# Attention, resampling, a GRU and a coupled oscillator on one core: where VectorE splits a block of weights, and how many selection matrices it builds before q and k

## The reference, cut to what matters

```python
x = x + attention(x, cond, ...)   # 16 heads of 32: rms norm, scale and shift by cond,
                                  # qkv, rms norm of q and k, softmax, o + o @ W_out
x = x + resample(x, cond)         # every output is w0*x[i0] + w1*x[i0+1], i0 and w1 from cond
x = x + gru(cond, x, ...)         # 64 steps, one after another
x = x + oscillator(cond, cond, x, ...)  # 64 steps of RK4, one after another
```

## Time and profile before

| | |
|---|---|
| median of three runs | 1607.8 us (1606.19, 1607.80, 1607.89) |
| the profiled execution, its own time | 1608.79 us |
| its span, first to last instruction | 1606.9 us |
| mean granted TensorE clock | 0.985 of full speed |
| PE busy | 1525.0 us, 95% of the span |
| DVE busy | 1361.6 us, 85% |
| ACT busy | 942.8 us, 59% |
| POOL busy | 685.1 us, 43% |

### The profile page before, as it was taken

One profiled execution on the slowest core, in us unless ns is written; L12 is line 12 of the kernel. 1 busy time (PEld: TensorE's weight loads), 2 busy tenths in 40 slices (PEclk: granted clock), 3 DMA queues, 4 the chain that ended last, 5 costly groups with the idle time before them and its releaser, 6 DMA issues.

```text
span 1606.9 us, 95997 instructions
## 1 busy us (share of the span) xinstructions
PE 1525.0 (95%) x42395; PEld 1356.1 (84%) x42395; DVE 1361.6 (85%) x3317; ACT 942.8 (59%) x2884; POOL 685.1 (43%) x851
## 2 busy tenths in 40 slices
PE   5799999999999999699999999999999999999995
PEld 3476767777777777699999999999999999999994
DVE  6778888888888887668999898988899998989897
ACT  6567677777766765245555555555555555555553
POOL 2335555544554553533433443343443443343331
PEclk8999999999999999899999999999999999999998
DMA  6111122222222213100000000000000000000000
GB/s 220 29 55 55 56 58 55 62 62 75 71 68 68 61 36 107 34 6 14 14 15 15 15 14 13 13 15 15 15 14 13 14 14 15 14 14 14 12 15 16
DMA packets 106658, 59.88 MB, mean 37 GB/s; under 512 B 77368, under 2 KB 91872, under 8 KB 106240
## 3 DMA queue, kind: packets, MB, share of 16 engines
q1 hardware_dynamic: 106144, 53.70, 13.0%
q10 hardware_dynamic: 96, 0.02, 0.0%
HBM read 33.71 MB, written 11.60 MB: 28 GB/s over the span
## 4 chain that ended last, share of the span: by engine, by line
PE 85%; DVE 8%; issue 5%; ACT 1%; DMA 0%; POOL 0%; ACTq 0%; DVEq 0%; POOLq 0%
PE psB L1365 33%; PE psA L1394 15%; PE psQ L1083 10%; PE psA L1399 7%; PE psQ L1124 7%; PE psO L1154 5%; PE psA L1092 2%; PE psO L1142 2%; PE psB L1106 2%; DVE first L716 1%; DVE front L724 1%; DVE first L719 1%; DVE room L737 1%; PE psQ L1179 0%; DVE PT L776 0%
## 5 line engine op out<-in xcount | busy, mean ns | idle before, releaser
L1365 PE MATMUL psB<-first,Wx 128*128 128x64 f16 x9216 | 292.3, 193 | 4.7 <-issue 3.8
L1394 PE MATMUL psA<-ts,Cp 128*128 128x64 f16 x8192 | 283.7, 193 | 11.5 <-ACT ts L1433 10.9
L1365 PE MATMUL psB<-first,Whh 128*128 128x64 f16 x9072 | 286.7, 193 | 0.9
L1365 PEld LDWEIGHTS psB<-first,Wx 128*128 128x128 f16 x9216 | 279.5, 98 | 5.8 <-issue 5.5
L1365 PEld LDWEIGHTS psB<-first,Whh 128*128 128x128 f16 x9072 | 273.9, 98 | 1.8 <-issue 1.7
L1083 PE MATMUL psQ<-Wx,front 128*128 128x512 f16 x1152 | 269.7, 384 | 4.6 <-DVE front L896 3.9
L1394 PEld LDWEIGHTS psA<-ts,Cp 128*128 128x128 f16 x8192 | 258.4, 98 | 13.1 <-ACT ts L1433 11.8
L1433 ACT ACTIVATE ts<-qst 128x256 f16<-128x256 f32 x192 | 80.1, 417 | 314.3 <-DVE qst L1536 314.3
L1083 PEld LDWEIGHTS psQ<-Wx,front 128*128 128x128 f16 x1152 | 111.3, 99 | 124.2 <-issue 7.1
L1399 PE MATMUL psA<-ts,Cp 128*128 128x64 f16 x4096 | 163.2, 194 | 0.3
L1674 POOL TENSOR_TENSOR en<-rz,dn 128x256 f32<-128x256 f32 x64 | 46.7, 729 | 257.0 <-issue 256.1
(11 more groups left out here) (187 smaller groups left out, 3008.1 us busy)
## 6 DMA issues: line engine op xcount, KB each, us to landing
front<-in_x SPq DMA_DIRECT2D x32, 256.0 KB, 2.7
rows<-rows_dram SPq DMA_DIRECT2D x64, 128.0 KB, 2.9
out<-ot SPq DMA_DIRECT2D x512, 16.0 KB, 1.8
x<-x SPq DMA_DIRECT2D x31, 224.0 KB
Whh<-in_L_cond_W_qkv SPq DMA_DIRECT2D x12, 256.0 KB, 7.6
room<-in_L_cond_W_hh SPq DMA_DIRECT2D x12, 256.0 KB, 2.9
room<-in_L_cond_W_ih SPq DMA_DIRECT2D x12, 256.0 KB, 2.8
wih_dram<-front SPq DMA_DIRECT2D x12, 256.0 KB, 3.0
```

Of the source, the lines that this page charges most:

```text
L1365: last = mm(o, W_[:, i, c, g * PART:(g + 1) * PART], src[:, j, c, :], start=False, stop=False, skip_group_check=True)
L1394: mm(psF[:, s % 2, m, :], Cp[:, i, c, m * PART:(m + 1) * PART], ts_[:, 0, c, :], start=(c == 0 and m == 0 and i == 0), stop=False, skip_gr ...
```

## The change

Two edits, both in the order of DVE's list in a slot. In slots 4 to 30 one chunk of the first selection matrix, where there were two, is built before `low_qk`, and three after it; in slot 3 none before it and four after it, so that the wait for the row of indices stands behind `low_qk` too. In slots 4 to 27 `low_wr` moves from the end of the slot to between the two calls of `weigh_taps`. Nothing is removed or added, and the list of the last slot and what follows it is the same.

```diff
             if p := pair(1):
                 scale_x(p)
-            if tap:
-                build(tap, 0, (0, 1))
+            if tap and tap.n > 0:
+                build(tap, 0, (0,))
             if p := pair(-1):
                 low_qk(p, 0)
                 low_qk(p, 1)
             if tap:
-                build(tap, 0, (2, 3))
+                build(tap, 0, (1, 2, 3) if tap.n > 0 else range(KC))
             sums_qk(qk, 0)
...
             if tap:
                 weigh_taps(tap, 0)
+            if 0 <= i - WR_FROM < WR_PIECES:
+                low_wr(i - WR_FROM)
+            if tap:
                 weigh_taps(tap, 1)
             if i == 3:
                 seeds()
-            if 0 <= i - WR_FROM < WR_PIECES:
-                low_wr(i - WR_FROM)
```

## The result

| | before | after |
|---|---|---|
| median | 1607.85 us (4 runs, 1606.19 to 1608.50) | 1584.72 us (4 runs, 1584.17 to 1593.25) |
| ratio of the runs | | 0.9883, 95% interval 0.9862 to 0.9904 |
| profiled execution | 1608.79 us, span 1606.9 | 1584.21 us, span 1582.4 |
| granted clock, mean | 0.985 | 0.986 |

The change makes the kernel faster by 1.17% with an interval of 0.96 to 1.38%: 18.8 us, 15.4 to 22.2. The forecast was 18.5 us less. The two medians differ by 23.1 us, more than the interval of the ratio allows. Two later comparisons, made with the experiments, gave 0.9882 (0.9866 to 0.9898) and 0.9867 (0.9837 to 0.9897), 19 to 21 us, with medians 19.05 and 19.62 us apart.

What follows compares the result with a forecast made beforehand. PE was taken to bound the slot but for a wait at the scores, set by DVE's path; 13.0 + 0.4 + 0.96 + 4.1 = 18.5 us less gave 1589.3 us, range 1586.8 to 1595.5.

Steps and rivals of the forecast that it cites:

- The path: DVE's chain from end of sampling to scores sets the slot; PE waits 0.54 us at the scores in 24 slots.
- The move of `low_wr`: Its 0.60 us falls into DVE's 0.99 us wait for the second sampling; alone worth 0.34 a slot, 8.2 us.
- Rival A: First chunk meets POOL's L415 or ACT's high halves are late; only `low_wr` pays: 12.7 us, 1595.1, chance 0.10.
- One chunk ahead: Moving the dear second chunk behind `low_qk` frees about 1.06 us; with both edits the whole wait goes, 13.0 us.
- PE's floor: The slot without PE's wait at the scores was taken as about 18.68 us.
- slot 4: Behind `seeds()`, PE's whole wait of 0.96 us goes, bounds 0.8 and 0.96.
- Slot 3: Wait for the row of indices hidden behind PE's work: 3.4 us, up to 4.8 if the clock stays up; middle 4.1.
- The chunks behind `low_qk`: Three chunks go at the ends of POOL's instructions; `low_p` and `mix` not delayed; costed at nothing.
- Rival C: Chunks behind `low_qk` shut out until POOL's row ends: 3.9 us a slot, 1713; chance 0.03 with anything else slower.
- Rivals B and D: B: another engine partly late, 1594 to 1595, chance 0.10; D: floor not 18.68, slot 3 alone gains, 1604, chance 0.03.
- The sum: 13.0 + 0.4 + 0.96 + 4.1 = 18.5 us less over the whole kernel, 1589.3 us.

Runs made afterwards that it cites:

- experiment 1: Only `low_wr` moved between the weighings, chunks as before, against the kernel before: 1598.57 us, ratio 0.9959.
- experiment 2: Only the chunks reordered, from slot 4 on, slot 3 and `low_wr` as before, against the kernel before: 1589.65 us, ratio 0.9901.
- experiment 9: Changed kernel with `low_wr` back at the end of the slot: 1585.96 us, ratio 0.9881 to the kernel before.
- experiment 8: Changed kernel with two chunks ahead of `scale_x` and two behind `low_qk`: 1586.66 us, one run.
- experiment 7: Changed kernel with the tap indices worked out before the sums of the probabilities in slot 2: 1582.66 us, again 1584.07; ratios 0.9849 and 0.9863 to the kernel before.
- experiment 3: Only slot 3's four chunks put behind `low_qk`, all else as in the kernel before: 1602.17 us, ratio 0.9981.
- experiment 4: The changed kernel run again, nothing altered, against the kernel before: 1585.79 us, ratio 0.9882.
- experiment 5: Changed kernel with no chunk ahead of `low_qk` in any slot, all four behind: 1587.42 us, ratio 0.9871 to the kernel before.
- experiment 10: Changed kernel with each block's split (`low_wr`) done twice between the weighings: 1589.57 us, one run, beside one of before at 1609.57.

## Why the prediction held, point by point

**The path.** "End of the sampling, weighing, `low_wr`, `scale_x`, chunks, `low_qk`, scores" was right: experiments 1 and 2 each take one link off it and the scores' wait shrinks by what was worked out (to 0.20) or vanishes.

**The move of `low_wr`.** 0.39 us of cover was forecast in the new place, 0.40 is there. The 0.34 us for it alone, 8.2 us in all, is what experiment 1's slots give. But the prediction stopped there and let the reader think that both edits fed the sum. They overlap: the chunks alone take the whole wait off (experiments 2 and 9), and the 0.34 us reappears as idling for ACT's high halves. The prediction's own numbers held this. With `scale_x` at its old 329.93, the lone chunk ends near 330.9, L719 near 332.2, ahead of the 332.71 at which PE is free. I placed the new order only with both edits in it. Rival A did not occur: the lone chunk took 0.34 us.

**One chunk ahead.** The dear second chunk is POOL's doing, shown by experiment 8. That agrees with the rule of the Trainium skill (SBUF — State Buffer, Practical consequences) that was named; the same section says that a VectorE instruction with two inputs in SBUF contends with a GpSimd instruction that reads SBUF, and experiment 7's L860, 2.27 us beside POOL's L400 and 0.68 without it, agrees too. That instruction was in the trace of before, at 2.27 us, and I had not looked at it.

**PE's floor: the mis-sized term.** I took 18.68 us, the old slot less its recorded wait. It is 18.61. When the scores wait, their first product doesn't start flush: the group costs 0.97 us in the chain of before and 0.90 in that of after, where it follows the projection's last product. The two lines of the chains:

```profile
333.25 0.97 PE psB L1106 x96
...
337.80 0.90 PE psB L1107 x96
```

So each removed wait is worth 0.07 more than its idle time, 0.61 and not 0.54, 0.27 and not 0.20: 15.2 us from S4 to S30 against the 13.4 of the sum, and 1.03 against 0.96 in slot 4.

**Slot 3.** 3.4 us for the wait was right (3.39). In experiments 1 and 2, whose slot 3 is that of before, S2 to S3 took 24.86 and 25.13 us and not 25.25, so the wait is worth 3.0 to 3.4, depending on the execution. For the clock I took the middle, 4.1 in all, with 4.8 as the upper value. The profiled execution kept its clock and gave 5.0, experiment 3's too; experiment 4's lost part of it and gave 4.2, experiment 5's 4.4. The upper value was 0.2 too low because I priced the scores and the turning of the probabilities at full clock and left out the weights of the taps right behind them, 0.69 us before and 0.46 after. "Nothing tells which" stands: the same wait of 1.72 us went both ways.

**The chunks behind `low_qk`.** Costed at nothing, and they cost nothing: DVE is free before `low_p`, with 0.23 us idle in the slot shown (0.3 forecast), and experiment 5 shows that a fourth chunk is free too. Rival C, chunks shut out for POOL's whole row of instructions, is refuted: the three chunks end at 339.57, in 2.34 us, while POOL goes on.

```profile
337.62 0.78 POOL L393 TENSOR_TENSOR um<-um 128x256 f32<-128x256 f32 x1
338.48 0.94 POOL L396 TENSOR_TENSOR XR<-XR,um 128x256 f32<-128x256 f32 x1
```

The last chunk ends 0.15 us after this L396, with five more instructions of the slot behind it on POOL's list. (Rival C counted seven behind the first L415; there are eight, L415 itself comes twice.) Rivals B and D didn't occur either.

**The sum.** With the floor and slot 3 as measured it is 21.3 us, not 18.5: 1.8 more for the floor, 0.9 for slot 3, 0.1 for slot 4. The ratios say 18.8, 18.9 and 21.3, all with intervals that hold 21.3. That 18.5 lies so near the first two is in part luck. My range was too narrow on its lower side, since it had bounds for slots 3 and 4 and none for the floor: 1607.8 less 21.3 is 1586.5, already 0.3 below its end. The median of the four runs lies 1.8 lower still. The profiled executions differ by 24.6, of which 3.2 came from parts that the change doesn't touch; those parts take 1053.1 to 1062.7 us together over the fourteen traces, so a difference of that size between two executions says nothing of the change.

## What to carry to other kernels

When two edits shorten the same path, place the new order with each of them alone as well: what ends the path next (here ACT's high halves, then PE itself) may make one of them worth nothing. A VectorE instruction that GpSimd's can block, as these comparisons, is cheap ahead of the instruction that releases GpSimd and dear once GpSimd has begun (about 0.3 us against 1.14 here), so order the list by who has been released. A wait for a transfer at the head of an in-order list should stand behind whatever doesn't need it, even if it is there only once: that one place gave about a fifth of this gain.

## What the runs showed of the hardware

**The clock after the same wait.** Nine traces have the wait of 1.72 to 1.87 us before the scores of slot 3, with the same instructions before it. In seven PE stayed at 2.4 GHz behind it; in two, those of experiments 4 and 5, it had gone back to work when it fell to 1.2 GHz, in the second microsecond after the start of the scores (mean 0.82 and 0.76 from 75 to 80 us), and it was back at 2.4 before the mixing. What decides between the two stays open.

**The last steps.** The recurrences, the same instructions in every kernel here, took 924.8 us in the trace of before, 923.2 in that of after, 919.5 in experiment 3's and 927.6 in experiment 10's. The last steps have little left for PE, and there the clock fell in some executions: it was 0.59 from 1552.4 to 1562.4 us of the changed kernel, and 1.00 over the same steps in experiment 3. The same group of products, in the changed kernel and then in experiment 3:

```profile
1557.44 1.89 PE L1395 MATMUL psA<-ts,Cp 128*128 128x64 f16 x32 [1.73 <-ACT ts L1434]
```

```profile
1572.27 1.11 PE L1394 MATMUL psA<-ts,Cp 128*128 128x64 f16 x32 [2.13 <-ACT ts L1433]
```

From the first such group that waits for ACT to the last it is 22.3 us in the changed kernel and 20.3 in experiment 3, so this explains 2 us of a spread of some 6 to 12 us between executions of one kernel. Experiment 1's trace kept the clock over these steps and took 924.6 us all the same. The rest, the one execution of 1593.25 us among it, of which there is no trace, stays open.
